# Another table of unit orders for the last rounds of a fused transformer kernel

## What is computed

```python
x = x + xattn(layernorm(x), ctx)   # self-attention, then attention over 257 context rows,
                                   # each + residual and layernorm; relu MLP; layernorm; relu
x = x + attn(layernorm(x))         # qkv = x @ W_attn, 16 heads of 32, causal softmax * decay, @ W_proj
x = x + ffn(layernorm(x))          # shared: ln(silu(x1) * x2) @ sw3
# ffn, for the rows named by index_b, index_t:
top1 = argmax(sigmoid(x_moe @ eg_w.T + eg_b) + exp_bias)
w = softmax([sigmoid(shared gate), expert score of top1])
out = shared_out * w[0] + expert_out[top1] * w[1]
```

## Time and profile before

| | us |
|---|---|
| median of 3 runs | 1475.81 (1474.77 to 1477.35) |
| time of the profiled execution | 1476.32 |
| its span | 1474.5 |
| PE busy | 1371.7 (93%) |
| DVE busy | 1133.4 (77%) |
| ACT busy | 586.0 (40%) |
| POOL busy | 523.8 (36%) |

### The profile page before, as it was taken

The page is one execution under the profiler, slowest core; times in us unless marked ns, Lnnn a source line. Parts: engine busy times, 40 slices in busy tenths (PEclk is TensorE's granted clock), DMA queues, the critical chain, the costliest instruction groups (busy, mean ns, idle before and its releaser), DMA issues.

```text
span 1474.5 us, 32944 instructions
## 1 busy us (share of the span) xinstructions
PE 1371.7 (93%) x13724; PEld 858.8 (58%) x13725; DVE 1133.4 (77%) x2349; ACT 586.0 (40%) x1108; POOL 523.8 (36%) x534
## 2 busy tenths in 40 slices
PE   7679999999999999999999999999999999998976
PEld 3355566656656666665666666666666666565533
DVE  5776678777788777877778787787777878777865
ACT  2543344444444444443444444444434444343221
POOL 0133334433434333343443433334334433333310
PEclk9899999999999999999999999999999999999989
DMA  9622444333333444433333344443333324435240
GB/s 349 250 95 107 144 144 144 135 105 116 134 105 128 143 144 144 144 139 108 114 136 106 119 144 144 144 143 141 118 108 131 120 104 144 144 137 222 81 164 22
DMA packets 38659, 201.38 MB, mean 137 GB/s; under 512 B 5096, under 2 KB 5992, under 8 KB 28400
## 3 DMA queue, kind: packets, MB, share of 16 engines
q1 hardware_dynamic: 37648, 198.93, 37.6%
q10 hardware_dynamic: 864, 0.36, 0.1%
HBM read 182.24 MB, written 17.04 MB: 135 GB/s over the span
## 4 chain that ended last, share of the span: by engine, by line
PE 67%; DVE 18%; issue 5%; POOL 4%; ACT 4%; DMA 1%; SPq 0%; DVEq 0%; POOLq 0%; ACTq 0%
PE ps_a L1638 10%; PE ps_a L1661 8%; PE ps_t L1661 8%; PE ps_t L1625 6%; PE ps_a L1647 6%; PE ps_a L1702 4%; PE ps_a L1673 4%; PE ps_v L1638 4%; PE ps_t L1638 3%; POOL rstd L622 3%; DVE stats L1105 3%; DVE arena L1236 3%; PE ps_t L1694 2%; PE ps_t L1673 2%; PE ps_t L1745 2%
## 5 line engine op out<-in xcount | busy, mean ns | idle before, releaser
L631 POOL TENSOR_TENSOR act_l<-act_t,act_h 128x512 f16<-128x512 f32 (+1 forms) x176 | 199.0, 1131 | 385.1 <-ACT act_t L746 222.8
L622 POOL TENSOR_TENSOR rstd<-var,mhalf 128x1 f32<-128x1 f32 x224 | 185.4, 828 | 301.8 <-DVE var L1107 301.2
L631 POOL TENSOR_TENSOR last_slot<-last_slot 128x512 f16<-128x512 f32 x80 | 89.5, 1118 | 168.3 <-ACT last_slot L746 97.4
L738 ACT ACTIVATE act_h<-ps_t,scale 128x512 f16<-128x512 f32 (+1 forms) x110 | 70.8, 644 | 156.3 <-PE ps_t L1625 156.3
L1661 PE MATMUL ps_a<-act_h,arena 128*128 128x128 f16 x1408 | 87.4, 221 | 18.0 <-ACT act_h L738 18.0
L1661 PEld LDWEIGHTS ps_a<-act_h,arena 128*128 128x128 f16 x1408 | 81.7, 99 | 28.3 <-ACT act_h L738 22.4
L1661 PE MATMUL ps_t<-act_h,arena 128*128 128x128 f16 x1408 | 88.0, 222 | 4.5 <-ACT act_h L738 4.5
L1661 PEld LDWEIGHTS ps_t<-act_h,arena 128*128 128x128 f16 x1408 | 82.4, 99 | 6.3 <-issue 2.9
L1638 PE MATMUL ps_a<-arena,act_h 128*128 128x512 f16 x352 | 83.4, 380 | 1.6 <-ACT act_h L738 1.6
L746 ACT ACTIVATE act_t<-ps_t,scale 128x512 f32<-128x512 f32 (+1 forms) x110 | 70.3, 639 | 34.8 <-PE ps_t L1625 34.8
L1236 DVE TENSOR_SCALAR arena<-ps_a,unscale 32x512 f32<-32x512 f32 x64 | 48.2, 754 | 43.7 <-PE ps_a L1673 42.5
(11 more groups left out here) (358 smaller groups left out, 3086.2 us busy)
## 6 DMA issues: line engine op xcount, KB each, us to landing
arena<-in_ctx_t SPq DMA_DIRECT2D x32, 2056.0 KB, 8.4
arena<-in_ctx_n SPq DMA_DIRECT2D x32, 2048.0 KB
ctx_last<-in_ctx_last SPq DMA_DIRECT2D x32, 256.0 KB
arena<-in_ew SPq DMA_DIRECT2D x8, 1024.0 KB, 6.1
x_in<-in_x SPq DMA_DIRECT2D x22, 256.0 KB, 7.2
x_scratch<-rows SPq DMA_DIRECT2D x22, 256.0 KB, 8.7
out<-rows SPq DMA_DIRECT2D x22, 256.0 KB, 2.0
arena<-in_ew SPq DMA_DIRECT2D x8, 512.0 KB, 7.3
```

The lines of the kernel that those rows point to most:

```text
L622: nc.gpsimd.tensor_tensor(rstd[s][:], var[s][:], mhalf[:], ALU.pow).then_inc(rstd_ready[s], 1)
L631: nc.gpsimd.tensor_tensor(act_l[s][:, chunks], act_t[s][:, chunks], act_h[s][:, chunks], ALU.subtract).then_inc(act_l_ready[s], 1)
L738: nc.scalar.activation(act_h[s][:, 0:width // P].rearrange("p c r -> p (c r)"), bank[s][:, 0:width], ACT.Copy, scale=scale[:, k:k + 1]).th ...
```

## The change

The diff:

```diff
--- before.py
+++ after.py
@@ -125,34 +125,34 @@
         (2, "turn_x2n"), (1, "out_norm"), (1, "turn_x1n"), (2, "silu"), (2, "turn_z")],
 }
 LAST = {
-    "pe": [(2, "project_k_l"), (3, "ffn_out"), (3, "ffn_out_l"), (1, "turn_pc"), (2, "project_q_l"), (2, "e_zt1"),
-        (1, "context_mix"), (2, "head_scores"), (2, "e_in3"), (0, "turn_xn"), (2, "project_v"), (2, "project_v_l"),
-        (1, "turn_w"), (2, "e_out1"), (0, "project_self"), (1, "e_turn"), (0, "project_self_l"), (1, "e_logits"),
-        (0, "value_self"), (1, "e_in0"), (0, "self_scores"), (2, "e_zt2"), (1, "context_out"), (1, "context_out_l"),
-        (0, "value_self_l"), (0, "turn_p"), (2, "head_mix"), (1, "e_in1"), (0, "self_mix"), (2, "e_out2"),
-        (2, "project_out"), (2, "project_out_l"), (1, "e_zt0"), (2, "e_zt3"), (2, "e_out3"), (1, "turn_h2"),
-        (1, "hidden"), (0, "turn_h"), (1, "hidden_l"), (1, "e_in2"), (0, "project_query"), (2, "turn_x2n"),
-        (1, "e_out0"), (0, "project_query_l"), (0, "context_scores"), (2, "ffn_in"), (2, "ffn_in_l"),
-        (1, "turn_x1n"), (1, "project_k"), (1, "project_q"), (2, "turn_z")],
-    "dve": [(3, "e_zn3"), (2, "e_zn0"), (2, "context_norm"), (2, "e_bias1"), (3, "project_out"), (2, "e_z1"),
-        (1, "self_norm"), (3, "x2_norm"), (2, "hidden"), (2, "out_norm"), (2, "x1_norm"), (3, "ffn_in"),
-        (1, "context_scores"), (3, "silu"), (3, "z_norm"), (3, "e_total"), (2, "e_zn1"), (2, "e_bias2"),
-        (2, "project_k"), (3, "ffn_out"), (0, "xn_moments"), (2, "e_z2"), (0, "turn_xn"), (1, "context_mix"),
-        (1, "context_total"), (1, "context_scaled"), (1, "e_moments"), (1, "e_norm"), (2, "head_scores"),
-        (1, "e_gate_a"), (2, "e_zn2"), (2, "head_total"), (0, "project_self"), (1, "e_gate_b"), (2, "head_weights"),
-        (1, "e_gate_c"), (1, "e_bias0"), (2, "e_bias3"), (0, "self_scores"), (2, "e_z3"), (1, "e_z0"),
-        (1, "context_out"), (0, "self_mix")],
-    "act": [(3, "head_mix_t"), (3, "head_mix"), (2, "turn_h2"), (2, "turn_h2_t"), (2, "e_zt0"), (2, "e_gate1"),
-        (1, "turn_h"), (3, "e_zt3"), (1, "turn_h_t"), (1, "project_query"), (3, "turn_x2n"), (3, "turn_x2n_t"),
-        (2, "turn_x1n"), (3, "ffn_in"), (2, "turn_x1n_t"), (1, "context_scores"), (3, "turn_z"), (3, "turn_z_t"),
-        (1, "turn_pc"), (2, "project_k"), (2, "project_q"), (1, "context_sum"), (0, "turn_xn_t"),
-        (1, "context_scaled"), (0, "turn_xn"), (2, "e_zt1"), (1, "turn_w_t"), (2, "e_gate2"), (1, "turn_w"),
-        (1, "e_turn"), (2, "head_scores"), (2, "project_v"), (0, "self_scores"), (0, "value_self"), (0, "turn_p"),
-        (1, "e_scores"), (1, "e_shares"), (1, "e_gate0"), (2, "e_zt2"), (2, "e_gate3")],
-    "pool": [(2, "turn_x1n"), (3, "silu"), (3, "turn_z"), (0, "xn_moments"), (0, "turn_xn"), (1, "e_norm"),
-        (2, "e_zn2"), (1, "turn_w"), (2, "head_scores"), (1, "e_zn0"), (2, "head_mix"), (2, "e_zn3"),
-        (1, "context_out"), (0, "self_mix"), (2, "project_out"), (1, "turn_h2"), (0, "turn_h"), (1, "e_zn1"),
-        (1, "hidden"), (2, "turn_x2n"), (1, "out_norm")],
+    "pe": [(3, "turn_z"), (2, "project_k_l"), (1, "turn_pc"), (2, "project_q_l"), (3, "ffn_out"), (1, "context_mix"),
+        (3, "ffn_out_l"), (2, "project_v"), (2, "head_scores"), (2, "project_v_l"), (1, "e_turn"), (0, "turn_xn"),
+        (1, "e_logits"), (0, "project_self"), (1, "e_in0"), (2, "e_out1"), (2, "e_zt2"), (0, "project_self_l"),
+        (0, "value_self"), (1, "turn_w"), (0, "self_scores"), (1, "context_out"), (1, "context_out_l"), (2, "e_in3"),
+        (2, "head_mix"), (0, "turn_p"), (0, "value_self_l"), (0, "self_mix"), (2, "project_out"), (1, "e_in1"),
+        (1, "turn_h2"), (2, "project_out_l"), (1, "hidden"), (1, "hidden_l"), (2, "e_out2"), (1, "e_zt0"),
+        (1, "e_in2"), (0, "turn_h"), (2, "turn_x2n"), (2, "e_zt3"), (0, "project_query"), (0, "project_query_l"),
+        (2, "ffn_in"), (1, "e_out0"), (0, "context_scores"), (2, "ffn_in_l"), (1, "turn_x1n"), (1, "project_k"),
+        (2, "e_out3"), (1, "project_q"), (1, "e_zt1")],
+    "dve": [(2, "hidden"), (2, "out_norm"), (3, "e_zn3"), (2, "x1_norm"), (2, "e_z1"), (3, "ffn_in"), (3, "silu"),
+        (1, "context_scores"), (2, "e_zn1"), (3, "z_norm"), (2, "e_bias2"), (2, "project_k"), (3, "e_total"),
+        (1, "context_total"), (1, "context_mix"), (2, "e_z2"), (3, "ffn_out"), (0, "xn_moments"), (1, "e_moments"),
+        (1, "context_scaled"), (1, "e_norm"), (0, "turn_xn"), (2, "head_scores"), (1, "e_gate_a"), (1, "e_gate_b"),
+        (2, "head_total"), (0, "project_self"), (2, "e_zn2"), (2, "head_weights"), (0, "self_scores"),
+        (1, "context_out"), (1, "e_gate_c"), (1, "e_bias0"), (1, "context_norm"), (2, "e_bias3"), (1, "e_z0"),
+        (0, "self_mix"), (2, "e_z3"), (1, "e_zn0"), (2, "project_out"), (0, "self_norm"), (1, "e_bias1"),
+        (2, "x2_norm")],
+    "act": [(2, "turn_h2_t"), (1, "turn_h"), (1, "turn_h_t"), (2, "e_zt0"), (3, "turn_x2n"), (1, "project_query"),
+        (3, "turn_x2n_t"), (2, "e_gate1"), (2, "turn_x1n"), (3, "ffn_in"), (3, "e_zt3"), (2, "turn_x1n_t"),
+        (3, "turn_z"), (1, "context_scores"), (2, "e_zt1"), (1, "turn_pc"), (3, "turn_z_t"), (2, "e_gate2"),
+        (2, "project_q"), (2, "project_k"), (1, "context_sum"), (1, "e_turn"), (0, "turn_xn"), (1, "e_scores"),
+        (0, "turn_xn_t"), (1, "context_scaled"), (2, "project_v"), (2, "head_scores"), (2, "e_zt2"), (2, "e_gate3"),
+        (1, "e_shares"), (1, "turn_w"), (1, "turn_w_t"), (0, "self_scores"), (0, "turn_p"), (0, "value_self"),
+        (2, "head_mix"), (2, "head_mix_t"), (1, "e_gate0"), (1, "turn_h2")],
+    "pool": [(3, "turn_z"), (0, "xn_moments"), (0, "turn_xn"), (1, "e_norm"), (2, "e_zn2"), (2, "head_scores"),
+        (1, "turn_w"), (1, "context_out"), (2, "head_mix"), (1, "e_zn0"), (0, "self_mix"), (2, "e_zn3"),
+        (1, "turn_h2"), (2, "project_out"), (0, "turn_h"), (1, "hidden"), (2, "turn_x2n"), (1, "out_norm"),
+        (1, "e_zn1"), (1, "turn_x1n"), (2, "silu")],
 }
 LOADS = [(0, "load_x"), (0, "set_first"), (0, "set_rest"), (0, "load_ctx_t"),
          (3, "store_x2"), (1, "e_first"), (1, "e_second"), (1, "e_rows"), (2, "e_fifth"), (3, "store"),
```

## The result

| | before | after |
|---|---|---|
| median | 1475.81 us | 1484.12 us (1482.16 to 1484.39, 5 runs) |
| ratio | | 1.005, 95% interval 1.0039 to 1.0061 |
| profiled execution, its span | 1476.32, 1474.5 us | 1484.12, 1482.3 us |
| PE busy | 1371.7 us | 1376.6 us |
| DVE, ACT, POOL busy | 1133.4, 586.0, 523.8 us | 1129.7, 585.8, 524.3 us |

The change makes the kernel 8.3 us slower by the two medians; the interval of the ratio allows 5.8 to 9.0 us. The forecast was 1473.7 us, and 1484.12 lies outside its range of 1469.3 to 1478.3, on the side that had a chance of 0.14.

A forecast was written before the change was run, and what follows sets the result against it. PE's stream sets the pace (busy 93%), and DVE's latency decides where PE stands still. Terms -0.3 + 1.9 - 3.7 = -2.1 us gave 1474.2 us against the profiled 1476.32, or 1473.7 as median; range 1469.3 to 1478.3 us.

The forecast's parts named there:

- Rounds 30 and 31: Waits of 2.5 us come before turn_xn, project_self and self_mix, 2.8 us of others go: net -0.3 us, in round 30.
- To e_turn: Round 32: x2 lands 0.6 us later, e_norm runs alone, -0.84 us; together e_turn comes 0.3 us early.
- The landing: Arrival of the x2 rows ahead of e_turn, requested after project_query_l(31): forecast 0.6 us later, still deciding when e_turn starts.
- From there to turn_x2n(31): From e_turn, new waits and lost cover turn 0.3 us ahead into 1.6 us behind: +1.9 us.
- the walk's +1.6: Sum of the forecast from round 30 to turn_x2n(31), without the tail's clock: -0.3 + 1.9 us.
- the tail's -3.7: After turn_x2n(31): e_out3 cuts PE's silence, so the clock stays full into the loop: -3.7 us, bounded by 0.
- -1.3: Tail, turn_z to the end of ffn_out_l: 2.7 us at full clock instead of 4.0.
- -2.4: The loop's first sixteen products: 6.9 us at full clock instead of 9.46.
- Rival 3: A second silence, before e_zt2, drops the clock during e_in3; tail's clock lost too: +3.3 us, 1479.1 us; chance 0.12.

The follow-up runs named there:

- e10: The changed kernel with useless products in PE's silences, half as many as the first filling, plus three ahead of the loop: 1474.95 us (0.999).
- e9: The kernel before with useless products in PE's silences, half as many as the first filling, plus three ahead of the loop: 1473.11 us (0.9973).
- e1: The changed kernel's new lists in rounds 30 and 31 only, the old LAST from round 32 on: 1477.25 us (1.0006).
- e2: The old lists in rounds 30 and 31, the changed kernel's new ones from round 32 on: 1480.32 us (1.0033).
- e4: The changed kernel with e_in3 moved ahead of e_zt2 on PE, into the wait of 2.54 us: 1486.94 us (1.0069).
- e12: The kernel before with only the load of the x2 rows issued ahead of the expert weights: 1472.89 us (0.9973).
- e7: The kernel before with ORDER kept up to round 31 and the x2 load issued ahead of the expert weights: 1468.31 us (0.9952).
- e5: The kernel before with the first, full number of useless products in PE's waits, none ahead of the loop: 1483.28 us (1.0048).
- e8: e7 with the useless products of e5, without those ahead of e_turn: 1473.5 us (0.9986).
- e11: e7 with half the useless products, one ahead of e_turn and three ahead of the loop: 1466.74 us (0.9933).

## Why the prediction was wrong

**Rounds 30 and 31: sign wrong, by 1.1 us.** Forecast -0.3, measured +0.77 (86.68 to 87.45). The waits came where they were put (0.30, 0.78, 0.87 us, for 0.65, 0.9, 0.9), and those before turn_h2 and hidden went; only turn_x2n kept a new one of 0.33 us. But the same instructions take 0.55 us more of PE's busy time in a round, 40.53 against 39.98 of rows 1. The two timelines of the round show it in many small steps from a unit's start to the next one's: project_k_l 1.18 us with turn_pc behind it for 0.89, project_v_l 1.04 for 0.86, hidden 1.88 for 1.74, project_query 1.91 for 1.78, context_mix 1.86 for 1.74. Whether these are waits too short to be shown or the price of other neighbours was not tried.

**To e_turn: the step right, its start wrong.** e_norm ran alone in 0.55 us, as forecast. The landing came 1.18 us later in the span, 1.63 if one counts that after reached the last unchanged units 0.45 us early; 0.6 was forecast, and the difference is the miss of the two rounds, carried on. So e_turn is 0.82 us late by the same count, for 0.3 early.

**From there to turn_x2n(31): right in sign without the clock.** The walk went from 0.3 us ahead to 1.6 behind, +1.9. In the filled kernels the two stages come to +0.91 us (0.88 and 0.03), with the rounds' +0.76 in all +1.67 for the walk's +1.6. That the sum fits is luck, since its two terms missed by 1.1 and by -1.0 us. The waits that I named stand in the trace: 0.81 before project_out, 1.29 before e_in1 (0.8 forecast), and 2.54 before e_zt2 (2.3 forecast).

**The clock: this is the step that failed.** The prediction has one clock term, the tail's -3.7, and puts the change of the clock everywhere else at nothing without a reason: e_in0, e_in3, the loop's later e_in and the last groups. The runs show +6.6 us in its place. Of the table's stages, (after - before) - (e10 - e9) is what the clock and the cover of it make, cover being waits for other engines that would have come anyway:

| | forecast | measured |
|---|---|---|
| to project_k(31) | 0 | 4.56 - 0.88 = +3.7 |
| to turn_x2n(31) | 0 | 1.70 - 0.03 = +1.7 |
| to the loop's first product | -1.3 | -0.23 + 0.03 = -0.2 |
| to the end | -2.4 | 1.45 - 0.02 = +1.4 |
| sum | -3.7 | +6.6 |

With the order's own +1.66, less the 0.45 us by which after was earlier at the start, that is the spans' difference, 7.8 us. Of the first row's 3.7 us, 0.4 lie ahead of e_turn, where the clock was at 1.00 in all four kernels, so they are not the clock's but a matter of when e_norm was done.

The -2.4 happened (9.46 to 7.13 us), but the later e_in of the loop took 5.92 us for 4.84, and the last two groups 1.72 and 3.76 us for 0.96 and 1.96. The -1.3 was not passed on: the loop's first product comes 2.2 us after POOL's last act_l in both kernels (1431.77 to 1433.99 and 1438.09 to 1440.34), and a faster ffn_out_l only lengthens the idle time marked "issue" from 0.60 to 1.59 us. Rival 3 named the right mechanism at the right place and even its price (e_in3 5.26 for 3.60: 1.7 us), but as an alternative with a chance of 0.12 and a point of decision at 2.7 us. It came at 2.54 us. That price is a quarter of the 6.6 us; the longer falls at e_in0 and in the loop and the new one over the last groups are in no rival.

**Why a fall cost more after than before.** Before, the fall of 1.7 us at e_logits and e_in0 cost 0.3, because DVE's chain ended the next waits anyway. In after it was 3.3 us long and cost all of it. So of the 3.3 us behind e_turn about half is the longer fall and half the lost cover. That the cover went by putting turn_w behind e_in0 and context_out right behind ACT's copy is read from the timelines and was not tested. The prediction costed silences and not what the work behind them covers; rival 3, too, took the fall at e_in0 for 1.7 us of time, of which e9 shows next to nothing.

**What stays open.** Why the clock falls at one wait and not at an equal one. Each kernel has one trace, and the clock is not the same in all executions of a kernel: over 85 runs of before the mean granted clock goes from 0.982 to 0.989, three at 0.989 took 1472.4 to 1472.7 us, and all at 0.982 took 1477.4 to 1478.3 us. So a stretch that fell in one trace and not in another may differ by the execution and not by the kernel, and no run tells the two apart. The sum is not in doubt, since all five runs of after (1482.16 us and up) are slower than all 85 of before (up to 1478.25), but how the 6.6 us divide between the stages holds for these two executions. How much of it another placement of the same lists would lose is open too: e1 and e2 share all their parts with before and after and fell at other places.

The prediction drew on the Trainium skill (TensorE: Matmul & The Clock Gate, What's actually happening), that activity releases the throttle. The traces agree in e9 and e10, where work in the silences kept the clock at 1.00 as long as PE had work. It speaks against the use that I made of it: work moved into a silence leaves one elsewhere, as in e4, where the lower clock came at project_out, though e4 too has but one trace.

## What to carry to other kernels

Where PE's clock falls behind silences, a reordering can cost several times what its waits do (8.3 us in all, 1.8 of them the order's own here). So a walk through the waits needs a range for the clock that takes in all the wide products behind its silences, with both signs. Measure the order with the silences filled before judging it. Look at the granted clock of several executions, not only at the profiled one. And before moving units around a wait, look at what starts its chain: one load issued ahead of a bulk of weights gave 0.27% alone and about 0.3% more on top of the ORDER table; the best list, ORDER in two rounds, gave 0.19%, which is not clear of it by the intervals.

## What the hardware showed that was not expected

Three pairs of stretches have the same PE units and the same waits, and a different clock in their one profiled execution each. e_turn waits 0.88 and e_logits 0.82 us in e12 and in e7, and e_in0 takes 3.68 us in the one and 6.69 in the other (PE's timelines, e12 first, with line numbers 3 higher):

```profile
1358.95 0.63 PE L1757 MATMUL ps_t<-ident,last_slot 128*128 128x128 f32 x4 [0.88 <-DVE last_slot L1386]
1360.40 1.03 PE L1763 MATMUL ps_e<-mask_self,last_slot 128*128 128x9 f32 x8 [0.82 <-ACT last_slot L842]
1361.28 3.68 PE L1788 MATMUL ps_a<-arena,last_slot 128*128 128x512 f32 x8
```

```profile
1353.66 0.63 PE L1757 MATMUL ps_t<-ident,last_slot 128*128 128x128 f32 x4 [0.88 <-DVE last_slot L1386]
1355.11 1.40 PE L1763 MATMUL ps_e<-mask_self,last_slot 128*128 128x9 f32 x8 [0.82 <-ACT last_slot L842]
1356.36 6.69 PE L1788 MATMUL ps_a<-arena,last_slot 128*128 128x512 f32 x8
```

e12's profiled execution is one of its four at 0.989, which took 1471.3 to 1471.9 us; its slowest, at 0.982, took 1476.5. The second pair is e_in3 behind the wait of 2.54 us in after and in e2 (5.26 and 3.60 us), the third the last groups of before and after behind the same 2.00 us (0.96 and 1.72 us for L1760).

PE's first product in the loop comes 2.2 to 2.3 us after POOL's last act_l in before, after, e2, e5, e9 and e10, whatever PE did until then; what those 2.2 us are was not tried.

Useless products paid: 4 us of before's time went away for 32 of them (64 matmuls in the trace), and no PE work of e9 ran at 0.50. Twice the filling took 10.2 us more (e5 against e9) and 6.8 us more (e8 against e11).
